# Gate and experts through tangents on ScalarE, and four more of 64 products with C on VectorE

## The chip, the cores and the metric

The kernel runs on one core of a Trainium2 chip. The metric is the device time of one execution in microseconds (us). Engines are named as the profile names them: PE is TensorE's matmul, PEld its weight load, DVE is VectorE, ACT is ScalarE, POOL is GpSimd, SP is SyncE, whose queue issues the transfers.

## The reference, cut to what matters

One layer of a decoder in three parts, each with a layer norm ahead of it and a residual sum behind it, on x of 64 x 128 x 512 floats: a state-space mixer, a banded cross attention, and a layer of eight experts. The mixer and the experts hold the silus that the change touches:

```
proj = einsum('blh,ph->blp', x, in_proj_w); h_in, gate = split(proj, 2)
u = silu(conv(h_in) + conv_b)                       # 1024 channels, 4 taps
ts, Bm, Cm = split(einsum('bli,pi->blp', u, x_proj_w))
dt = softplus(einsum('blr,ir->bli', ts, dt_proj_w) + dt_proj_b)
h[t] = exp(dt[t] * A) * h[t-1] + dt[t] * u[t] * Bm[t]    # 16 states a channel
y = einsum('blin,bln->bli', h, Cm) + D * u
y = y * silu(gate)
x = x + einsum('bli,hi->blh', y, out_proj_w)
...
h = einsum('bth,eih->beti', x, down_w)
a = silu(h)                                         # 8 experts of 16 units
out = einsum('beth,bte->bth', einsum('beti,ehi->beth', a, up_w), top2_gate)
```

## The kernel before

The 64 batch rows are worked off in 32 groups g of two rows (GB = 2). Every engine has a list written out by hand, `iteration(g, cur, nxt, p1, p2)`, which holds four things at once: the scan part of the mixer for group g (`cur`), the preparation of group j = g + 1 (`nxt`: layer norm, input products, taps, u, time step), the attention of group g - 1 (`p1`) and the experts of group g - 2 (`p2`). Engines meet only through semaphores, so an instruction that waits holds up all that stands behind it in its own list. A loop runs two iterations at a time; the first, the second and the last ones are written out, `first_iteration` and `last_iteration` among them.

The scan part of a group has 64 steps s. Step s is channel block ic = s // 8 (128 channels) and state pair r = s % 8; it works on 128 x 512 floats (two states, two rows, 128 time steps):

- `decays(g, s)` on ACT (L564): two exponents of delta times A into one of two PSUM banks (DAR = 2). The soft steps (softplus) use the same two banks in turn. `bank_free` lets it wait until the bank's last user is done: the scan (`h_done`), or, where the product with C is DVE's, that product (`hcd_done`). In that case ACT must also write the first columns anew (L561).
- `times_b(g, s)` on POOL (L351): du times B into one of eight slots of `ring`; it waits until PE has summed what stood in the slot (`hc_used`), at a group's start also for `du_done` and for the transfer `bc_in`.
- `scan(g, s)` on DVE (L1789): the recurrence. Its result goes into the ring, or for steps in `DVE_C` into the PSUM bank.
- `times_c`: the product with C, on POOL for most steps (L360), on DVE (L1773) for those in `DVE_C`, now 16 of 64: s % 8 in (1, 5).
- `y_sum(g, s)` on PE (L1321): transposes two finished slots and adds them up in bank PS_Y; `y_step` on DVE (L1782) multiplies the sum of a channel block by the gate; `y_turn` on PE (L1342) transposes it back into PS_B, and `y_back` on ACT (L658) copies it to `yz`, which `out_proj` (L1351) uses.

Bank PS_B is shared, one user at a time: `h_in` (L1371) with `tap3` on ACT and `conv` on DVE (L1895), `gate_in` (L1394) with the gate's copy, `dt_in` (L1429), `ts_in`, `bc_in_rows`, `transposed_x` and `y_turn`. Each next user waits on PE for the semaphore of the last reader. For the gate that is `gate_done`, which `h_in`, `transposed_x`, `dt_in` and `y_turn` wait for.

Today the gate (quarters q = 0 to 3 of its channels) is copied raw by `gate_raw` (L683) and turned in two halves by `gate_silu` (L689) beside the silus of u (L676). The experts' silu is L743, their product with the weights L1795. `soft_step` 1 to 4 on DVE (L1757 to L1768) with `soft_exp`, `soft_one`, `soft_ln`, `soft_back` on ACT make softplus; step 4 makes `du`. The tiny powers of the layer norms are POOL's (L339), the shifts that use them DVE's (L1745).

## Time and profile before

| | us |
|---|---|
| median of 3 runs | 4900.89 (4900.83 to 4907.75) |
| profiled execution | 4886.05 |
| its span | 4884.2 |

| engine | busy us | share of the span |
|---|---|---|
| PE | 4537.1 | 93% |
| PEld | 3339.0 | 68% |
| POOL | 4505.7 | 92% |
| ACT | 4281.4 | 88% |
| DVE | 4252.6 | 87% |

Busy time is the union of an engine's instructions in one profiled execution. The ends of matmuls are modelled, so a busy PE may hold waits. The span runs from the first to the last instruction. Releasers are inferred from semaphore events: a wait is put down to the instruction that signalled last. Since the kernel repeats one group 32 times, most of what there is to see is in one group, and windows are cut at the first product of a group on POOL.

### The profile page before, as it was taken

The page shows a single profiled execution, that of the slowest core. Times are in us where ns is not written, and L with a number is a line of the kernel's source. Part 1 is how long each engine was busy: PE and PEld are TensorE (multiplying, and loading weights), DVE is VectorE, ACT ScalarE, POOL GpSimd, SP SyncE. Part 2 cuts the span into 40 slices and gives each one's busy share as a digit, 9 for nine tenths or more (in the row PEclk, how much of TensorE's full clock was granted, in tenths as well). Part 3 has the DMA queues.
Part 4 walks back from the last instruction along what each step waited for, and adds up shares of the span by engine and source line. Part 5 has one row for each costly group of instructions (what it writes and reads, how often), then busy time and mean ns, then how long its engine had stood idle before and what let it go on. Part 6 is the DMA issues. An engine that isn't in the chain of part 4 may idle for free.

```text
span 4884.2 us, 142078 instructions
## 1 busy us (share of the span) xinstructions
PE 4537.1 (93%) x52548; PEld 3339.0 (68%) x52548; DVE 4252.6 (87%) x5795; ACT 4281.4 (88%) x9026; POOL 4505.7 (92%) x3726
## 2 busy tenths in 40 slices
PE   5799999999999999999999999999999999999977
PEld 4576767776767776767767676777667777677754
DVE  3788989899988899988899988899989899888883
ACT  5788999988999988999988999988999989999873
POOL 3999999999999999999999999999999999999991
PEclk8899999999999999999999999999999999999999
DMA  3211222212222212222212222212222212222200
GB/s 127 80 55 64 77 80 79 84 49 73 77 79 80 84 47 75 77 79 79 84 40 82 77 79 80 84 38 84 77 80 79 84 35 88 77 79 80 71 8 19
DMA packets 119316, 350.46 MB, mean 72 GB/s; under 512 B 18688, under 2 KB 19456, under 8 KB 118528
## 3 DMA queue, kind: packets, MB, share of 16 engines
q1 hardware_dynamic: 118656, 341.51, 20.3%
q8 instruction: 432, 7.08, 0.6%
q14 instruction: 228, 1.87, 0.1%
HBM read 323.64 MB, written 17.83 MB: 70 GB/s over the span
## 4 chain that ended last, share of the span: by engine, by line
PE 41%; POOL 34%; issue 12%; DVE 8%; DMA 2%; ACT 1%; POOLq 0%; SPq 0%; DVEq 0%; ACTq 0%
POOL ring L351 21%; POOL ring L360 12%; PE ps L1321 8%; PE ps L1371 7%; PE ps L1394 6%; DVE ring L1789 3%; PE ps L1351 3%; DMA bc<-bc_rows 2%; PE ps L1210 2%; PE ps L1276 2%; PE ps L1265 2%; PE ps L1237 2%; DVE nmax L1813 2%; PE ps L1301 2%; DVE hc L1895 1%
## 5 line engine op out<-in xcount | busy, mean ns | idle before, releaser
L351 POOL TENSOR_TENSOR ring<-du,bc 128x512 f32<-128x512 f32 x2048 | 2581.9, 1288 | 205.1 <-PE ps L1321 109.4
L360 POOL TENSOR_TENSOR ring<-ring,bc 128x512 f32<-128x512 f32 x1536 | 1947.2, 1290 | 48.3 <-DVE ring L1789 42.4
L1789 DVE TENSOR_TENSOR_SCAN ring<-ps,ring 128x512 f32<-128x512 f32 x1536 | 1828.8, 1211 | 184.3 <-ACT ps L564 154.3
L564 ACT ACTIVATE ps<-delta,a_neg 128x254 f32<-128x254 f32 x4096 | 1760.7, 469 | 159.2 <-DVE ring L1789 150.4
L1321 PE MATMUL ps<-ident,ring 128*128 128x128 f32 x8192 | 1073.8, 277 | 54.2 <-POOL ring L360 51.7
L1321 PEld LDWEIGHTS ps<-ident,ring 128*128 128x128 f32 x8192 | 914.8, 142 | 208.2 <-issue 140.4
L1789 DVE TENSOR_TENSOR_SCAN ps<-ps,ring 128x512 f32<-128x512 f32 x512 | 622.7, 1216 | 70.7 <-ACT ps L564 47.8
L1371 PE MATMUL ps<-xt_a,w_in 128*128 128x256 f32 x2048 | 477.0, 386 | 16.6 <-ACT yz L658 14.8
L1394 PE MATMUL ps<-w_in,xt_a 128*128 128x256 f32 x2048 | 472.6, 384 | 4.2 <-ACT delta L617 3.0
L726 ACT ACTIVATE probs_mem<-ps 128x768 f32<-128x768 f32 x504 | 443.1, 912 | 30.4 <-PE ps L1265 21.4
L1351 PE MATMUL ps<-w_outp,yz 128*128 128x512 f32 x1024 | 465.8, 593 | 2.7 <-issue 1.5
L1371 PEld LDWEIGHTS ps<-xt_a,w_in 128*128 128x128 f32 x2048 | 382.5, 192 | 82.3 <-ACT yz L658 22.5
L1394 PEld LDWEIGHTS ps<-w_in,xt_a 128*128 128x128 f32 x2048 | 384.1, 191 | 77.5 <-issue 24.2
L1895 DVE SCALAR_TENSOR_TENSOR hc<-ps,conv_w,hc 128x254 f32<-128x254 f32 (+2 forms) x768 | 362.2, 475 | 46.1 <-ACT hc L669 26.1
L1813 DVE TENSOR_REDUCE nmax<-ps 128x8 f32<-128x1280 f32 x252 | 371.5, 1474 | 30.5 <-PE ps L1237 29.0
L1773 DVE TENSOR_TENSOR ring<-ps,bc 128x512 f32<-128x512 f32 x512 | 350.3, 684 | 8.0
L1351 PEld LDWEIGHTS ps<-w_outp,yz 128*128 128x128 f32 x1024 | 182.4, 190 | 173.3 <-issue 171.5
L1237 PE MATMUL ps<-qk 32*32 32x160 f32 (+2 forms) x16128 | 289.5, 295 | 0.0
L1265 PE MATMUL ps<-qk 32*128 32x192 f32 x4032 | 262.0, 374 | 0.0
L1210 PE MATMUL ps<-xb,w_qk 128*128 128x512 f32 x504 | 241.8, 602 | 11.9 <-ACT xb L595 11.7
L1276 PE MATMUL ps<-probs_mem,v_aug 128*32 128x192 f32 x4032 | 218.9, 358 | 14.5 <-ACT probs_mem L726 14.3
L1237 PEld LDWEIGHTS ps<-qk 32*32 32x32 f32 x16128 | 198.0, 103 | 37.3 <-issue 0.6
(174 smaller groups left out, 6280.7 us busy)
## 6 DMA issues: line engine op xcount, KB each, us to landing
w_in<-in_w_in SPq DMA_DIRECT2D x256, 512.0 KB, 3.6
bc<-bc_rows SPq DMA_DIRECT2D x256, 512.0 KB, 5.9
x_new<-in_x SPq DMA_DIRECT2D x32, 512.0 KB, 8.1
x_res<-in_x SPq DMA_DIRECT2D x32, 512.0 KB, 7.6
out<-x_att SPq DMA_DIRECT2D x32, 512.0 KB, 2.9
enc<-in_ctx SPq DMA_DIRECT2D x63, 256.0 KB, 3.4
w_outp<-in_w_outp SPq DMA_DIRECT2D x1, 2048.0 KB, 7.9
bc_rows<-bc_sb SPq DMA_DIRECT2D x128, 8.0 KB, 1.4
```

Source lines behind the costliest of these rows:

```text
L351: nc.gpsimd.tensor_tensor(ring[:, s % RING, :].rearrange("p (n t) -> p n t", n=2), du[:, q % 2, (ic % 2) * NT:(ic % 2 + 1) * NT].rearrange ...
L360: nc.gpsimd.tensor_tensor(ring[:, s % RING, :], ring[:, s % RING, :], bc[:, s % RS, 2:4, :].rearrange("p a t -> p (a t)"), ALU.mult).then_ ...
L564: nc.scalar.activation(ps[:, bank("step", s), (n % 2) * NT:(n % 2 + 1) * NT].rearrange("p (b t) -> p b t", b=GB)[:, :, 1:T], delta[:, ic, ...
L726: nc.scalar.activation(L.probs[:, :, blk, lo:hi], ps[:, L.bank:L.bank + 4, (n % 2) * WIN + lo:(n % 2) * WIN + hi], ACT.Exp).then_inc(L.p_d ...
L1237: last = nc.tensor.matmul(ps[32 * a:32 * a + 32, L.bank + hp, j * NEAR + lo:j * NEAR + hi], L.qk[r:r + 32, j, n * P + 32 * a:n * P + 32 * ...
L1321: last = nc.tensor.matmul(ps[:, PS_Y, b * T:(b + 1) * T], ring[:, t % RING, n * NT + b * T:n * NT + (b + 1) * T], ident[:], start=False, s ...
L1351: last = nc.tensor.matmul(ps[:, PS_ATT + b, :], yz[:, ic, b * T:(b + 1) * T], w_outp[:, ic, :], start=(ic == 0), stop=(ic == NI - 1))
L1371: last = nc.tensor.matmul(ps[:, prep_bank(j, "h", q), a * NT:(a + 1) * NT], w_in[:, slot, k, a * P:(a + 1) * P], xt_a[:, k, :], start=(k = ...
L1394: last = nc.tensor.matmul(ps[:, PS_B, b * NT:(b + 1) * NT], xt_a[:, k, b * T:(b + 1) * T], w_in[:, slot, k, :], start=(k == 0), stop=(k == ...
L1789: nc.vector.tensor_tensor_scan(state, ps[:, bank("step", s), :], ring[:, s % RING, :], 0.0, ALU.mult, ALU.add).then_inc(h_done, 1)
L1813: nc.vector.tensor_reduce(L.nmax[:, n].rearrange("p j (a r) -> p a j r", r=32)[:, :, :, DH], ps[:, L.bank:L.bank + 4, 0:NJ * NEAR].rearran ...
L1895: nc.vector.scalar_tensor_tensor(acc[:, :, s:T], src[:, :, 0:T - s], conv_w[:, ic, KC - 1 - s:KC - s], acc[:, :, s:T], ALU.mult, ALU.add). ...
```

## The change

1. The gate: `gate_raw` and `gate_silu` go. ACT's `gate_tanh(j, q)` writes tanh(gate / 2) from PS_B into `gate_t`, and DVE's new `gate_half(j, q)` makes (tanh + 1) * gate from it and PS_B. That is twice the silu, so `y_back` halves it. `gate_done` is now signalled by `gate_half`.
2. The experts: `experts_tanh` and `experts_half` in the same way, and `experts_gated` carries the factor 0.5.
3. `DVE_C` has 20 of 64 steps, s % 16 in (1, 5, 9, 11, 13), in place of 16: steps 11, 27, 43 and 59 move from POOL to DVE.
4. The lists of POOL, ACT, PE and DVE are ordered anew. SP's list is the same.

```diff
-    DVE_C = [s for s in range(64) if s % 8 in (1, 5)]
+    DVE_C = [s for s in range(64) if s % 16 in (1, 5, 9, 11, 13)]
...
-                nc.scalar.copy(yz[:, ic, :], ps[:, PS_B, 0:NT]).then_inc(yz_done, 1)
+                nc.scalar.activation(yz[:, ic, :], ps[:, PS_B, 0:NT], ACT.Identity, scale=0.5).then_inc(yz_done, 1)
...
-            def gate_raw(j, q):
+            def gate_tanh(j, q):
 
                 reached(act, y_done, (j - 1) * NI + 2 * q + 2)
                 act.wait_ge(gin_ps, j * NQ + q + 1)
-                nc.scalar.copy(gate_t[:, :, 2 * q * P:(2 * q + 2) * P],
-                               ps[:, PS_B, :].rearrange("p (b c) -> p b c", b=GB)).then_inc(gate_done, 1)
-
-            def gate_silu(g, h):
-                act.wait_ge(gate_done, g * NQ + 2 * h + 2)
-                z = gate_t[:, :, 4 * h * P:4 * (h + 1) * P]
-                nc.scalar.activation(z, z, ACT.Silu).then_inc(gate_act, 1)
+                nc.scalar.activation(gate_t[:, :, 2 * q * P:(2 * q + 2) * P],
+                                     ps[:, PS_B, :].rearrange("p (b c) -> p b c", b=GB), ACT.Tanh, scale=0.5).then_inc(gate_act, 1)
...
-                nc.scalar.activation(act_e, ps[:, PS_ATT + 2, 0:NT], ACT.Silu).then_inc(act_done, 1)
+                nc.scalar.activation(act_e, ps[:, PS_ATT + 2, 0:NT], ACT.Tanh, scale=0.5).then_inc(act_tanh, 1)
...
+            def gate_half(j, q):
+
+                dve.wait_ge(gate_act, j * NQ + q + 1)
+                z = gate_t[:, :, 2 * q * P:(2 * q + 2) * P]
+                nc.vector.scalar_tensor_tensor(z, z, 1.0, ps[:, PS_B, :].rearrange("p (b c) -> p b c", b=GB),
+                                               ALU.add, ALU.mult).then_inc(gate_done, 1)
+
...
-                dve.wait_ge(gate_act, g * 2 + ic // 4 + 1)
+                dve.wait_ge(gate_done, g * NQ + ic // 2 + 1)
...
+            def experts_half(g):
+
+                dve.wait_ge(act_tanh, g + 1)
+                nc.vector.scalar_tensor_tensor(act_e, act_e, 1.0, ps[:, PS_ATT + 2, 0:NT], ALU.add, ALU.mult).then_inc(act_done, 1)
+
...
-                nc.vector.tensor_tensor(gated, ps[:, PS_ATT + 3, 0:NT], act_e, ALU.mult).then_inc(gated_done, 1)
+                nc.vector.scalar_tensor_tensor(gated, ps[:, PS_ATT + 3, 0:NT], 0.5, act_e, ALU.mult, ALU.mult).then_inc(gated_done, 1)
```

Of the lists, what the prediction speaks of. Start of an iteration on POOL (in the new order the power "e" of group g - 2 stands behind three products) and on DVE (y_step 7 comes first, the shifts later):

```diff
                 if cur:
                     times_b(g, 0)
-                if p2:
-                    rstd("e", g - 2, 0, 2)
-                if p1:
-                    second_lane(g)
-                if cur:
                     times_b(g, 1)
                     times_b(g, 2)
+                if p2:
+                    rstd("e", g - 2, 0, 2)
...
-                if p2:
-                    shift("e", g - 2, 0)
+                if p1:
+                    y_step(g - 1, 7)
                 if cur:
                     scan(g, 0)
                     scan(g, 1)
                 if p2:
-                    shift("e", g - 2, 1)
+                    shift("e", g - 2, 0)
```

The end of an iteration on DVE:

```diff
                 if p1:
                     attention(g, 1, "x2")
+                if cur:
+                    scan(g, 63)
                 if nxt:
                     soft_step(1, j, 0)
-                if cur:
-                    scan(g, 63)
-                if nxt:
                     soft_step(2, j, 0)
                     soft_step(3, j, 0)
                     soft_step(4, j, 0)
+                    gate_half(j, 2)
```

On DVE the new instructions stand so: `gate_half(g, 3)` between soft step 4 of quarter 1 and scan 6; `experts_half` between the two parts of `router`; `gate_half(j, 0)` between soft steps 1 and 2 of quarter 3, behind `times_c` 33; `gate_half(j, 1)` between scan 43 and the third maximum of lane 1; the products with C of steps 11, 27, 43 and 59 behind mixer_add 1, y_step 2, the third maximum and scan 59. On ACT, `gate_tanh(g, 3)` stands ahead of decays 6, `gate_tanh(j, 0)` behind `soft_one(g, 3)`, `gate_tanh(j, 1)` right ahead of the silus of u, and `gate_tanh(j, 2)` behind `soft_ln(j, 0)`, with the next exponents behind it.

## Rows read from the trace of the kernel before

**Rows 1.** The page: busy time by engine, and the chain that ended last by engine.
```profile
PE 4537.1 (93%) x52548; PEld 3339.0 (68%) x52548; DVE 4252.6 (87%) x5795; ACT 4281.4 (88%) x9026; POOL 4505.7 (92%) x3726
...
PE 41%; POOL 34%; issue 12%; DVE 8%; DMA 2%; ACT 1%; POOLq 0%; SPq 0%; DVEq 0%; ACTq 0%
```

**Rows 2.** Busy by stage: stretch, length, PE, PEld, DVE, ACT, POOL; clock; DMA.
```profile
4772.00:4884.00 112.00, 86.10 (x1178) 50.77 (x1178) 34.60 (x77) 42.78 (x68) 7.09 (x10) 0.92 0.06 20
...
sum 1174.70, PE 1121.90 PEld 827.93 DVE 1061.41 ACT 1068.28 POOL 1125.53; mean PE 140.24 PEld 103.49 DVE 132.68 ACT 133.54 POOL 140.69
...
2175.00:2228.00 53.00, 51.74 (x634) 39.46 (x626) 49.53 (x68) 46.27 (x94) 48.75 (x41) 1.00 0.14 41
```

**Rows 3.** Waits of POOL in eight groups, 1396 to 2570.7: total us, times, longest.
```profile
POOL ring L351 <- PE ps L1321: 27.0, 24, 1.6
POOL ring L360 <- DVE ring L1789: 11.4, 16, 1.3
POOL ring L351 <- DVE du L1768: 8.4, 9, 0.9
```

**Rows 4.** Waits of DVE in the same eight groups.
```profile
DVE ring L1789 <- ACT ps L564: 34.5, 37, 2.9
DVE ln_nm_e L1745 <- POOL ln_rs_e L339: 17.7, 8, 2.2
...
DVE ps L1789 <- ACT ps L564: 11.3, 16, 0.8
```

**Rows 5.** Timeline over one group: POOL's products, and last three scans on DVE.
```profile
2129.71 1.27 POOL L351 TENSOR_TENSOR ring<-du,bc 128x512 f32<-128x512 f32 x1 [0.94 <-DVE du L1768]
...
2131.60 6.19 POOL L351 TENSOR_TENSOR ring<-du,bc 128x512 f32<-128x512 f32 x5
...
2276.36 1.27 POOL L351 TENSOR_TENSOR ring<-du,bc 128x512 f32<-128x512 f32 x1 [0.94 <-DVE du L1768]
...
2219.16 3.45 DVE L1789 TENSOR_TENSOR_SCAN ring<-ps,ring 128x512 f32<-128x512 f32 x3
```

**Rows 6.** Groups of instructions, whole run: count, busy us, mean ns, idle before.
```profile
L360 POOL TENSOR_TENSOR ring<-ring,bc 128x512 f32<-128x512 f32 x1536 | 1947.2, 1290 | 48.3 <-DVE ring L1789 42.4 <-PE ps L1321 4.6 <-issue 1.3
L1789 DVE TENSOR_TENSOR_SCAN ring<-ps,ring 128x512 f32<-128x512 f32 x1536 | 1828.8, 1211 | 184.3 <-ACT ps L564 154.3 <-POOL ring L351 27.0
...
L1773 DVE TENSOR_TENSOR ring<-ps,bc 128x512 f32<-128x512 f32 x512 | 350.3, 684 | 8.0
...
L561 ACT COPY ps<-zeros 128x4 f32<-128x4 f32 x640 | 105.3, 164 | 18.0 <-DVE ring L1773 16.5
...
L633 ACT ACTIVATE ps<-soft 128x512 f32<-128x512 f32 x128 | 76.3, 596 | 5.8 <-DVE ring L1789 2.8
...
L683 ACT COPY gate_t<-ps 128x512 f32<-128x512 f32 x128 | 73.2, 572 | 7.5 <-PE ps L1394 7.4
...
L689 ACT ACTIVATE gate_t<-gate_t 128x1024 f32<-128x1024 f32 x64 | 63.9, 1048 | 0.0
...
L1831 DVE SCALAR_TENSOR_TENSOR o_sb<-ps,enc 128x512 f32<-128x512 f32 x63 | 43.0, 682 | 26.9 <-PE ps L1301 26.9
...
L743 ACT ACT_TABLE_LOAD x32 | 41.1, 1283 | 0.6
...
L564 ACT ACT_TABLE_LOAD x157 | 201.4, 1283 | 2.8
```

**Rows 7.** Timeline of ACT in the same group: gate copy, silus of the gate, load back.
```profile
2205.14 0.59 ACT L683 COPY gate_t<-ps 128x512 f32<-128x512 f32 x1
...
2226.88 1.99 ACT L689 ACTIVATE gate_t<-gate_t 128x1024 f32<-128x1024 f32 x2
...
2228.95 1.28 ACT L564 ACT_TABLE_LOAD   x1
```

**Rows 8.** Chain of waits in order of time: start, us, what (PE, same group).
```profile
2199.49 3.46 PE ps L1394 x16
...
2206.49 3.46 PE ps L1371 x16
```

More of the change, by code:

```diff
@@ L961, in iteration @@
                     u_silu(j, 3)
+                if cur:
+                    y_back(g, 4)
+                    decays(g, 51)
+                    decays(g, 52)
                 if p1:
@@ L1629, in iteration @@
                 if p1:
+                    attention(g, p2, 1, "rep")
+                if nxt:
+                    dt_in(j, 2, cur)
+                if p1:
+                    attention(g, p2, 1, "wo")
+                if cur:
+                    y_sum(g, 59)
+                    y_turn(g, 6, nxt)
+                if p1:
                     attention(g, p2, 1, "ct")
-                if cur:
-                    y_turn(g, 6, nxt)
-                    y_sum(g, 59)
                 if nxt:
@@ L2055, in iteration @@
                 if cur:
-                    times_c(g, 41)
-                    scan(g, 42)
+                    y_step(g, 4)
+                    scan(g, 43)
+                if nxt:
+                    gate_half(j, 1)
                 if p1:
```

537 lines of the change are left out of this document (258 added, 279 removed).

## The prediction

> **What bounds the kernel now.** The page comes first: four engines are busy for 87 to 93% of the span, and the chain that ended last lies 41% on PE and 34% on POOL [rows 1]. No single engine stands out there, because the start and the end of the run are in the average. So the second view is the busy time by stage, cut at the starts of the groups on POOL. The reader is to see that a group of two batch rows takes 146.8 us (1174.70 over 8), with POOL 140.7, PE 140.2, ACT 133.5 and DVE 132.7 us busy in it, and that only the last 112 us are of another kind [rows 2]. The timeline of POOL confirms the period: the first product of two consecutive groups starts at 2129.71 and at 2276.36 [rows 5]. 32 groups make 32 x 146.8 = 4698 us of the 4884; the rest is start and tail.
>
> The third view is who POOL waits for. Over eight groups it is 27.0 + 11.4 + 8.4 us, under 6 us a group: PE freeing a ring slot, DVE ending a scan, DVE ending `du` [rows 3]. POOL's own work is fixed: five products in a row take 6.19 us and one takes 1.27, so they start (6.19 - 1.27) / 4 = 1.23 us apart [rows 5], and 112 of them a group (64 with B, 48 with C) are 137.8 us. So POOL runs from product to product nearly without a break and is the bound of the steady stretch. PE is a close second: between 2175 and 2228 us it is busy for 51.7 of 53 us [rows 2]. But PE's ends are modelled, and its stretches with waits count in part as busy, so I take its 140.2 as an upper bound of its need.
>
> The fourth view is who DVE waits for: it idles 14.1 us a group, of which (34.5 + 11.3) / 8 = 5.7 us are scans that wait for ScalarE's decays and 2.2 us the shift that waits for POOL's power at the start of a group [rows 4].
>
> **The change, part by part, for one group.**
>
> *POOL loses four products with C* (steps 11, 27, 43, 59): 4 x 1.23 = 4.9 us, 140.7 - 4.9 = 135.8. As POOL is the bound, all of it lies on the path until another engine takes over.
>
> *DVE gets those four*, at 0.68 us each (L1773) [rows 6]: 2.7 us. The scan before each writes to PSUM and not to the ring, which I cost at nothing. It gets four `gate_half`, 128x512 from SBUF and PSUM. The nearest row is the product with the context, the same form and size, 0.68 us (L1831) [rows 6]: 2.7 us. And it gets one `experts_half`, half the size: between half of L1831 and the whole, 0.34 to 0.68; I take 0.4. Together 5.9 us by durations. Three scans in a row take 3.45 us and not 3 x 1.21 [rows 5], so each instruction behind another costs some 0.09 less than its duration: 9 x 0.09 = 0.8 off, and 5.1 is the other end. I take 5.7: DVE goes from 132.7 to 138.4.
>
> *ScalarE loses* two `gate_silu` of 1.05 us, 2.1 (L689), and the two table loads about the experts' silu, one before it (L743, 32 in the run, one a group) and one back to the exponent (L564, 157 in the run, five a group): 2 x 1.28 = 2.6 [rows 6]. The gate's silus sat between loads that `u_silu` needs anyway, so those stay. It gains next to nothing where a copy becomes an activation: four times 572 to at most 596 ns (L683, L633), 0.1; eight `y_back` likewise, 0.1 to 0.2. And it must set the first column of the decays' bank four more times, after each new product on DVE: 4 x 0.16 = 0.7 (L561) [rows 6]. ScalarE: 133.5 - 4.7 + 0.9 = 129.7.
>
> In this trace a load costs its 1.28 us and no more: the load back at 2228.95 stands right behind the gate's silus, which began at 2226.88 and ran 1.99 us, to 2228.87 [rows 7], and the 32 loads ahead of the experts' silu have 0.6 us of idle time in front of them in all [rows 6]. So the sum goes by 1.28. The Trainium skill, "ScalarE: Activation LUTs", What ACT_TABLE_LOAD costs, adds a drain of about 1.38 us to each switch of tables, by which the two switches would be worth an estimated 5.3 us and ScalarE would stand near 127. The trace disagrees with it.
>
> *The waits that are added.* The gate's sum must now stay in PS_B until DVE has multiplied it, where ScalarE's copy freed the bank before. `gate_done` is DVE's now, and PE's next user of the bank (`h_in`, `transposed_x`, `dt_in`, `y_turn`) waits for it. Queued behind a waiting `gate_half` on DVE are the scans, behind them POOL's products with C. The price of each is at least the 0.68 us of the instruction on the bank's chain and at most that and one scan in front of it, 1.9 us; four a group, 2.7 to 7.6 us on PS_B. What hides it is PE's other work (attention and `y_sum` use other banks), and with that cover I take nothing; without it the full price lands on PE. The new product on DVE also holds a PSUM bank of decays for 0.68 + 0.16 us longer before ScalarE can fill it. In the order on DVE something stands between each such pair (a maximum, an addition, a `y_step`), which covers it. A gain from these waits is excluded, since they only hold banks longer.
>
> *The order.* On DVE scan 63 now stands ahead of all four soft steps, where one stood ahead of it: the first product of the next group waits for `du` 0.94 us now [rows 5], and scan 63 and the steps come in the same total, so I expect 0 to 0.7 us more. POOL's power "e" moves behind three products and DVE's shift moves behind two scans, which gives back a part of the 2.2 us wait [rows 4]. These cancel, within 1 us. On SP nothing is moved; its spreads wait for the same steps' last use, 59 now on DVE. Start and tail: no silu of the gate in the first group, `gate_in` 2 later there, one table load fewer in the tail; between -2 and +2 us in all, taken as 0.
>
> **The sum.** The heaviest engine falls from POOL's 140.7 to DVE's 138.4, with POOL at 135.8 right below. The bound engine now idles 146.8 - 140.7 = 6.1 us a group. If the new one idles as long, the period is 138.4 + 6.1 = 144.5, which is 2.3 us less; 32 x 2.3 = 74 us. That asks DVE's idle time to fall from 14.1 to 6.1 us, and 5.7 of that are waits for ScalarE, which has lost 3.8 us of work and the two longest interruptions in their present size. The profiled execution took 4886.05 us around a span of 4884.2; 4886 - 74 = 4812. The median of the runs stands 14.8 us above the profiled one, so the forecast for the median is **4826 us**.
>
> **The rivals.**
>
> *POOL's saving comes through whole.* For it: DVE and ScalarE are waited for by POOL little today (19.8 us in eight groups [rows 3]), and DVE's 138.4 still fits under 141.9. Against: DVE would have 3.5 us of idle time a group, where it has 14.1. Time: 32 x 4.9 = 157, 4901 - 157 = 4744. Chance 0.17.
>
> *Nothing comes of it.* Of DVE's 14.1 us of idle time, 8.4 are not waits for ScalarE. If these are not slack but real latencies (PE to maximum, POOL to shift), the period is 138.4 + 8.4 = 146.8, as today; PE's full stretch from 2175 to 2228 us would end the same way, since PE loses no work. Time: 4901. Chance 0.10.
>
> *Slower, through the bank PS_B.* The place is PE's full stretch. `gate_in` of gate 0 starts there at 2199.49 and runs 3.46 us; `h_in` 2, the next user of the bank, starts at 2206.49 [rows 8], and ScalarE's copy between them ran from 2205.14 to 2205.73 [rows 7], 0.8 us ahead of it. A `gate_half` behind the tangent takes the bank to 2206.4 at best, and to 2207.6 with a scan in front of it; gate 1 falls into the same stretch and is taken as equally tight. In this stretch PE's halts go through to POOL, which already waits most for PE [rows 3]. At the upper price the two gates cost 2 x 1.9 = 3.8 us a group, while the saving of 2.3 is felt only in the other 94 of 147 us, 1.5. So it decides from 0.75 us a gate, and in full it gives 2.3 us more a group: 4901 + 74 = 4975. Against it: PE's other banks give it work, if the order puts it there. Chance 0.10.
>
> *The tangent doesn't share the decays' table.* Then the change doesn't do what it says: each lone tangent brings a load in and one back. Gate 0, gate 3 and the experts stand alone, six loads, and gate 2 between logarithm and exponent makes one more; above the forecast's count that is 7 x 1.28 = 9 us a group, 129.7 + 9.0 = 138.7 on ScalarE, beside a DVE of 138.4 that waits for it. With ScalarE's idle time of 146.8 - 133.5 = 13.3 us kept, the period is 152.0: 4901 + 32 x 5.2 = 5067. No row has a tangent, so none decides; other functions, such as the reset and the gate's copy (L561, L683) [rows 6, 7], run among the exponents without a load, while silu and logarithm bring one. Chance 0.04. The Trainium skill, "ScalarE: Activation LUTs", Table sets: the hidden batching unit, lists tanh in the set of exp, by which no load is added; no row of this trace shows it.
>
> **How the numbers follow.** The forecast's own case has 0.59, with a range of its own of 4773 to 4879 (DVE at 137.8 to 138.6, idle time of the bound engine 5 to 7.5 us, so a period of 142.8 to 146.1). The whole range goes from 4740, which takes in the first rival, to 4905, which takes in "nothing comes of it"; outside are the two slow cases, 0.14, and the tails of the others. A measurement of this kernel can tell about 0.2%, 10 us, from no change. Faster: 0.59 + 0.17 = 0.76, and 0.01 of "nothing comes of it", which leaves 0.09 for the same; slower: 0.10 + 0.04 = 0.14.
>
> **What would show it.** In the profile after: L360 with 1408 products instead of 1536, DVE's product with C with 640; POOL at 135.8 us a group; ScalarE's loads down by 64 in all and its busy time near 130; DVE near 138.4 and the largest of the three. Right is the forecast if DVE's waits for ScalarE fall to some 2 us a group and POOL's idle time rises to 8 or 9. It is wrong if POOL's waits for PE grow (the bank), if DVE shows long waits ahead of `gate_half`, or if loads appear at the tangents' line.

## The result, and the profile after

The kernel after takes 4931.38 us (median of 4 runs, 4930.73 to 4933.95), the one before 4900.86: a ratio of 1.007 (95% interval 1.0054 to 1.0085). It is slower, and outside the range of the prediction. In the profiled executions the spans are 4928.9 and 4884.2 us, 44.7 apart; the profiled execution of before was some 15 us shorter than its median, so these rows show about 15 us more than the medians do.

Those 15 us go with TensorE's granted clock. The profiled execution of before has a mean of 0.989. Of 62 further executions of before, made beside the runs below, five stand at 0.988 and took 4882 to 4894 us; 0.985 is the commonest value, with 4893 to 4905 us; three stand at 0.983, with 4901 to 4907. So the usual execution of before loses time to the clock that its trace does not show. The kernel after took 4931 to 4934 us at 0.982 to 0.983. At a like clock the change costs some 25 us, an estimate (4931 against 4907 at 0.983), and only the other 5 or 6 of the 30.5 come from a clock that is lower than before's usual one.

The page of the kernel after: busy time, the chain that ended last, and the groups that answer to [rows 6].

```profile
PE 4565.9 (93%) x52548; PEld 3373.7 (68%) x52548; DVE 4397.6 (89%) x6083; ACT 4184.7 (85%) x9025; POOL 4353.3 (88%) x3598
...
PE 44%; DVE 17%; POOL 16%; issue 14%; ACT 7%; DVEq 0%; DMA 0%; POOLq 0%; ACTq 0%; SPq 0%
...
L351 POOL TENSOR_TENSOR ring<-du,bc 128x512 f32<-128x512 f32 x2048 | 2566.6, 1278 | 302.8 <-PE ps L1299 191.9
L360 POOL TENSOR_TENSOR ring<-ring,bc 128x512 f32<-128x512 f32 x1408 | 1778.0, 1278 | 128.4 <-DVE ring L1772 127.1
...
L1749 DVE TENSOR_TENSOR ring<-ps,bc 128x512 f32<-128x512 f32 x640 | 437.8, 684 | 8.0
...
L558 ACT COPY ps<-zeros 128x4 f32<-128x4 f32 x768 | 126.8, 165 | 122.2 <-DVE ring L1749 117.5
```

The counts are those of the change (1408 and 640 products with C), and POOL, 34% of the chain in [rows 1], is down to 16%, while DVE went from 8 to 17%. Lines shifted: the scan is L1772 now, the decays L561, `y_sum` L1299, `gate_half` L1757, the tangent L680.

Busy time by stage, cut at the starts of groups on POOL, as in [rows 2]: two groups of eight, and the sum.

```profile
1848.30:1997.60 149.30, 141.76 (x1643) 105.29 (x1642) 137.18 (x190) 130.52 (x283) 135.94 (x112) 0.99 0.22 74
1997.60:2145.40 147.80, 140.36 (x1643) 103.62 (x1642) 137.34 (x190) 130.68 (x283) 136.00 (x112) 1.00 0.22 73
...
sum 1188.20, PE 1128.47 PEld 835.62 DVE 1097.83 ACT 1045.14 POOL 1087.84; mean PE 141.06 PEld 104.45 DVE 137.23 ACT 130.64 POOL 135.98
```

A group takes 148.5 us, where it took 146.8 [rows 2]. The work of each engine is close to the forecast: POOL 136.0 (135.8), DVE 137.2 (138.4), ScalarE 130.6 (129.7), PE 141.1 (140.2, as before). POOL's load fell by 4.7 us and the group got longer. But the heaviest load hardly fell: it is PE's now, 140.3 in the short groups, where POOL's was 140.7. So the error lies in the idle time, and in which engine counts as the bound. And the groups alternate, 149.3 and 147.8, with 1.4 us more busy time on PE in the long ones.

Who waits in these eight groups of the kernel after (1254.3 to 2442.5), answering to [rows 3, 4]: total us, times, longest.

```profile
POOL ring L351 <- PE ps L1299: 47.9, 43, 2.4
POOL ring L360 <- DVE ring L1772: 33.4, 45, 1.7
POOL ring L351 <- DVE du L1744: 14.3, 8, 1.8
...
DVE ring L1772 <- ACT ps L561: 34.6, 36, 2.2
DVE gate_t L1757 <- ACT gate_t L680: 11.5, 16, 0.8
DVE ps L1772 <- ACT ps L561: 10.9, 8, 1.6
...
PE ps L1159 <- DVE nmax L1801: 16.7, 16, 1.7
```

POOL's waits grew by three quarters for PE (27.0 to 47.9), tripled for DVE's scans (11.4 to 33.4) and rose for `du` (8.4 to 14.3). DVE's waits for the decays are what they were: 34.6 + 10.9 against 34.5 + 11.3. PE's waits for a maximum come to the same total as before, but in 16 pieces of up to 1.7 us and not 32 of up to 1.0; this row of the kernel before (1396 to 2570.7) is:

```profile
PE ps L1181 <- DVE nmax L1813: 17.4, 32, 1.0
```

The long groups are explained by TensorE's clock. Busy time of after in stretches of 3.4 us, some 39 us into a long group (the last three columns are the granted clock, the DMA share and GB/s).

```profile
2177.80:2181.20 3.40, 3.31 (x86) 2.69 (x88) 3.40 (x7) 3.37 (x9) 3.02 (x3) 1.00 0.18 67
2181.20:2184.60 3.40, 1.66 (x96) 0.99 (x75) 3.40 (x4) 3.24 (x8) 3.40 (x4) 1.00 0.27 96
2184.60:2188.00 3.40, 3.40 (x37) 3.14 (x16) 3.40 (x4) 2.15 (x5) 3.40 (x4) 0.50 0.00 0
```

And PE in the timeline of the same place:

```profile
2180.51 1.17 PE L1215 MATMUL ps<-qk 32*32 32x128 f32 x64
2183.42 0.32 PE L1159 MATMUL ps<-band,ident 32*128 32x320 bf16 x4 [1.74 <-DVE nmax L1801]
```

PE waits 1.74 us for a maximum, is busy for 1.66 of 3.40 us, and right behind that the granted clock is 0.50, so 1.2 instead of 2.4 GHz, for 3.4 us. In the trace of after this happens in 14 of 27 steady groups; in that of before never. The wait itself is in all 27 groups, 1.74 to 1.75 us each time, so the wait alone does not decide whether the clock falls.

### The profile page after: what moved, and what is told of

It is laid out like the page before. It is cut to its first block, busy times and chain, and to the rows that moved or that the text cites. A ratio compares the mean times of both kernels' runs of the same rounds, so it can differ in the third digit from the quotient of the medians.

```text
span 4928.9 us, 142489 instructions
## 1 busy us (share of the span) xinstructions
PE 4565.9 (93%) x52548; PEld 3373.7 (68%) x52548; DVE 4397.6 (89%) x6083; ACT 4184.7 (85%) x9025; POOL 4353.3 (88%) x3598
## 4 chain that ended last, share of the span: by engine, by line
PE 44%; DVE 17%; POOL 16%; issue 14%; ACT 7%; DVEq 0%; DMA 0%; POOLq 0%; ACTq 0%; SPq 0%
POOL ring L351 10%; PE ps L1299 8%; PE ps L1349 7%; POOL ring L360 6%; PE ps L1372 5%; PE ps L1215 4%; DVE ring L1772 4%; DVE ps L1772 3%; PE ps L1243 3%; PE ps L1254 2%; PE ps L1188 2%; DVE nmax L1801 2%; PE ps L1329 2%; ACT ps L561 2%; DVE ring L1749 1%
## 5 line engine op out<-in xcount | busy, mean ns | idle before, releaser
L360 POOL TENSOR_TENSOR ring<-ring,bc 128x512 f32<-128x512 f32 x1408 | 1778.0, 1278 | 128.4 <-DVE ring L1772 127.1
L561 ACT ACTIVATE ps<-delta,a_neg 128x254 f32<-128x254 f32 x4096 | 1757.4, 467 | 134.1 <-DVE ring L1772 122.5
L1772 DVE TENSOR_TENSOR_SCAN ring<-ps,ring 128x512 f32<-128x512 f32 x1408 | 1671.4, 1211 | 152.4 <-ACT ps L561 143.8
L1299 PE MATMUL ps<-ident,ring 128*128 128x128 f32 x8192 | 1080.8, 280 | 36.0 <-POOL ring L360 32.5
L1299 PEld LDWEIGHTS ps<-ident,ring 128*128 128x128 f32 x8192 | 948.7, 144 | 114.5 <-issue 100.1
L1772 DVE TENSOR_TENSOR_SCAN ps<-ps,ring 128x512 f32<-128x512 f32 x640 | 778.2, 1216 | 52.7 <-ACT ps L561 49.7
L1749 DVE TENSOR_TENSOR ring<-ps,bc 128x512 f32<-128x512 f32 x640 | 437.8, 684 | 8.0
L558 ACT COPY ps<-zeros 128x4 f32<-128x4 f32 x768 | 126.8, 165 | 122.2 <-DVE ring L1749 117.5
```

What stands on the lines that cost most here:

```text
L360: nc.gpsimd.tensor_tensor(ring[:, s % RING, :], ring[:, s % RING, :], bc[:, s % RS, 2:4, :].rearrange("p a t -> p (a t)"), ALU.mult).then_ ...
L561: nc.scalar.activation(ps[:, bank("step", s), (n % 2) * NT:(n % 2 + 1) * NT].rearrange("p (b t) -> p b t", b=GB)[:, :, 1:T], delta[:, ic, ...
L1299: last = nc.tensor.matmul(ps[:, PS_Y, b * T:(b + 1) * T], ring[:, t % RING, n * NT + b * T:n * NT + (b + 1) * T], ident[:], start=False, s ...
L1749: nc.vector.tensor_tensor(ring[:, s % RING, :], ps[:, bank("step", s), :], bc[:, s % RS, 2:4, :].rearrange("p a t -> p (a t)"), ALU.mult). ...
L1772: nc.vector.tensor_tensor_scan(state, ps[:, bank("step", s), :], ring[:, s % RING, :], 0.0, ALU.mult, ALU.add).then_inc(h_done, 1)
```

## The experiments

Two theories from the comparison. **T1**: the tangents hold the bank PS_B for DVE, and PE, nearly full, loses what it waits (the prediction's third rival). **T2**: POOL was not the only bound; its relief turns into waits, and what is lost comes from the order of the work and what it does to PE (the clock). "Group" is the mean of the steady groups 3 to 29 of the profiled execution; "falls" is how many falls of the clock those 27 groups hold; the last column is the mean of those of the 27 that hold none, and how many they are. Each ratio is against the executions of before that were made beside that run, whose medians lie between 4896.5 and 4901.9 us.

The expectations name their theories anew. BANK is T1; ORDER, CLOCK and LATENCY are forms of T2; and "theory DVE" is a third, that every microsecond of work given to DVE lengthens the group.

| run | median us | ratio to before (95%) | group us | falls | us without a fall |
|---|---|---|---|---|---|
| before | 4900.9 | 1 | 146.80 | 0 | 146.80 (27) |
| after | 4931.4 | 1.0070 (1.0054 to 1.0085) | 148.55 | 14 | 147.86 (13) |
| tangents_alone | 4980.3 | 1.0167 (1.0147 to 1.0187) | 149.71 | 1 | 149.64 (26) |
| c20_alone | 4903.1 | 1.0011 (1.0002 to 1.0021) | 147.26 | 0 | 147.26 (27) |
| tangents_c20_old_order | 5046.6 | 1.0310 (1.0293 to 1.0327) | 152.06 | 9 | 151.50 (18) |
| after_c16 | 5060.5 | 1.0329 (1.0307 to 1.0351) | 152.51 | 32 | 150.77 (5) |
| new_lists_silus | 5194.5 | 1.0601 (1.0584 to 1.0619) | 156.99 | 54 | none |
| experts_tangent | 4899.3 | 1.0000 (0.9989 to 1.0010) | 147.19 | 5 | 146.78 (22) |
| after_no_dip | 4984.0 | 1.0174 (1.0153 to 1.0195) | 150.09 | 2 | 150.06 (25) |
| after_filled | 4911.6 | 1.0031 (1.0018 to 1.0043) | 147.77 | 0 | 147.77 (27) |
| before_light_pe | 4866.0 | 0.9929 (0.9909 to 0.9948) | 146.22 | 24 | 144.60 (3) |
| after_light_pe | 4860.1 | 0.9922 (0.9905 to 0.9938) | 146.08 | 17 | 145.36 (10) |
| tangents_light_pe | 4848.3 | 0.9897 (0.9880 to 0.9915) | 145.78 | 1 | 145.67 (26) |
| c20_light_pe | 4970.9 | 1.0143 (1.0118 to 1.0167) | 150.02 | 77 | none |
| after_short_half | 4927.5 | 1.0059 (1.0042 to 1.0076) | 148.43 | 13 | 147.74 (14) |
| after_light_short | 4838.0 | 0.9871 (0.9855 to 0.9887) | 145.70 | 16 | 144.90 (11) |
| after_no_silu_load | 4905.6 | 1.0017 (1.0006 to 1.0028) | 147.67 | 13 | 147.05 (14) |
| before_no_silu_load | 4891.8 | 0.9988 (0.9978 to 0.9997) | 147.00 | 4 | 146.70 (23) |
| filled_c59_back | 4915.3 | 1.0045 (1.0029 to 1.0062) | 147.78 | 0 | 147.78 (27) |
| filled_c59_scan63 | 4932.2 | 1.0078 (1.0058 to 1.0098) | 148.26 | 0 | 148.26 (27) |

Of the 18 runs behind the first two, five came out in a range that was named for them (experts_tangent, tangents_c20_old_order, after_light_pe, after_short_half, before_no_silu_load) and two within 5 us of a named time (after_filled, filled_c59_back). The other eleven lie outside every range named, so neither theory had the sizes right.

### The parts of the change, each by itself

**The tangents in the order of before.** The functions of the change, each `gate_half` at its place among DVE's old neighbours, 16 products with C (on ScalarE the second tangent stands one place earlier than the copy did, ahead of the first silu of u):

```diff
-                    gate_raw(j, 0)
+                    gate_tanh(j, 0)
...
-                    gate_silu(g, 1)
-                if nxt:
-                    gate_silu(j, 0)
...
                     scan(g, 43)
+                if nxt:
+                    gate_half(j, 1)
```

> Kernel of before with its own lists and its own 16 products with C on DVE; only the silus of gate and experts become tangents with gate_half and experts_half. Theory DVE (each microsecond of work given to DVE lengthens the group, whatever the others lose): DVE 132.7 + 3.0, ScalarE 133.5 - 4.3, POOL stays at 140.7, so the group stays within 1 us of 146.8, 4880 to 4930. Theory ORDER (the parts are good, the new lists lose the time): ScalarE's two loads fewer shorten the waits of the scans, and the group falls by 0.5 to 1.5 us, 4855 to 4885.

They cost 1.7%. Waits of PE in eight groups of tangents_alone (1276.5 to 2473.2):

```profile
PE ps L1361 <- DVE gate_t L1771: 18.6, 16, 1.6
PE ps L1171 <- DVE nmax L1815: 18.1, 32, 1.0
```

`h_in`, the next user of PS_B, waits for `gate_half` twice a group, 18.6 / 8 = 2.3 us, of the 2.9 us by which the group is longer. That is T1, at the place that the prediction's third rival names and inside its price of 1.9 us a gate. How much of it is the hold of the bank and how much the place of `gate_half` behind other work of DVE, no run separates: `gate_half` was never shortened in this order.

**The four products in the order of before** (each behind its scan on DVE, gone from POOL's list):

```diff
-    DVE_C = [s for s in range(64) if s % 8 in (1, 5)]
+    DVE_C = [s for s in range(64) if s % 16 in (1, 5, 9, 11, 13)]
```

> Kernel of before with silus as they are and its own lists; only the products with C of steps 11, 27, 43 and 59 go from POOL to DVE, each right behind its scan. Theory DVE: POOL 140.7 - 4.9, DVE 132.7 + 2.7 = 135.4, the scans wait longer for decays that wait for the product: group 147 to 149 us, 4905 to 4970. Theory ORDER: the bound engine gets 4.9 us shorter and the group falls by 1 to 3 us, 4805 to 4870.

Busy time and POOL's waits of c20_alone in eight groups (1251.3 to 2429.3):

```profile
sum 1178.00, PE 1122.42 PEld 827.54 DVE 1080.97 ACT 1071.51 POOL 1086.93; mean PE 1122.42 PEld 827.54 DVE 1080.97 ACT 1071.51 POOL 1086.93
...
POOL ring L351 <- PE ps L1317: 56.8, 36, 2.6
POOL ring L360 <- DVE ring L1785: 25.9, 32, 1.2
```

POOL is at 1086.93 / 8 = 135.9 us, 4.8 less, and not one microsecond comes out: the group is 0.5 us longer. POOL's waits grew from 27.0 + 11.4 to 56.8 + 25.9, by 44.3 / 8 = 5.5 us a group. So POOL was no bound by itself: other chains are as long. T2's first half is shown. The ratio of 1.0011 flatters the run: it has no fall and a clock of 0.988 to 0.990 in its executions, which took 4899 to 4907 us, where before took 4882 to 4894 at 0.988.

**Both in the order of before.** The change without its new order:

> The kernel before with the whole change but its order: tangents, gate_half behind what they need, C products of steps 11, 27, 43, 59 on VectorE right behind their scans, all else as before. Tangents alone cost 79 us and the four products alone 2. Theory 1, the loss is in the hold of the bank PS_B, which the products don't touch: 4980 to 4990. Theory 2, the two add up worse, because DVE gets both works and gate_half then waits behind a product with C too (0.7 us a gate more on the bank's chain): 5000 to 5080. Rival, POOL's relief takes up a part of the tangents' loss: 4930 to 4960, and then the new order is worth nothing; by theories 1 and 2 it is worth 50 to 150 us.

The two add up to more than their sum: 3.1% against 1.7 + 0.1. So the new order is worth 5047 - 4931 = 115 us against this kernel. It is not the cause of the loss as a whole, it hides most of it. It does so at the bank too: here PE waits for `gate_half` 102 us at `h_in` over the whole run, and in after once there, for 0.7 us, and three times in all:

```profile
PE ps L1407 <- DVE gate_t L1757: 2.8, 1, 2.8
PE ps L1349 <- DVE gate_t L1757: 0.7, 1, 0.7
PE ps L1372 <- DVE gate_t L1757: 0.3, 1, 0.3
```

**The new order without one part.** The four products given back to POOL (11 behind B 17, the others beside their neighbours with C):

> Kernel after with the four products with C back on POOL (steps 11, 27, 43, 59, each put where a free ring slot needs it), all else as after. POOL 140.9, DVE 134.6. Theory DVE: no gain is lost with the four, the group comes back to 146 to 148 us, 4880 to 4925. Theory ORDER: POOL's work comes on top of the stalls that the new lists make, group 149 to 152, 4945 to 5040.

And the silus back in the new order, with `gate_raw` at the tangents' places and `gate_silu` twice behind `u_silu`:

> Kernel after with its new lists and its 20 products with C on DVE, but gate and experts with silus as before (gate_raw at the places of gate_tanh, the two gate_silu behind the silus of u). DVE 135.4, ScalarE 134.2, POOL 135.8. Theory BANK: the new lists are made to cover the hold of PS_B, so without it they gain little, and ScalarE's loads come back: 4920 to 4960. Rival, theory DVE: 3 us less on DVE shorten the group by 1 to 3 us, 4835 to 4900.

Both are far slower than after. In after_c16 PE's `y_sum` waits for POOL's products, which it hardly did:

```profile
PE ps L1303 <- POOL ring L360: 24.3, 16, 2.2
```

In the new order the four products are worth 129 us, and nothing in the old one. A part of it is TensorE's clock, which falls 32 and 54 times in the 27 groups of these two. So the products have no price of their own outside an order.

The other run says less. In new_lists_silus DVE's `y_step` waits for the silu of the gate, 24.6 and, put down to "issue", 24.2 us in eight groups (1300 to 2556), 6.1 us a group, and in before it did not:

```profile
DVE yg L1768 <- ACT gate_t L686: 24.6, 4, 6.2
DVE yg L1768 <- issue: 24.2, 4, 6.1
```

In this run that silu stands behind decays 44, in before behind decays 42. So its 5.3% over after are in large part the place that the silu was given, and whether the new order suits silus stays open.

**The experts' tangent alone**, in the order of before:

> Kernel of before with its lists; only the experts' silu becomes a tangent on ScalarE and experts_half on DVE, so the two table loads go and the bank PS_B, which only the gate uses, is held no longer. Theory BANK (the tangents lose by the longer hold of PS_B alone: with them PE waits 2.3 us a group for gate_half): no loss here, ScalarE 2.6 us lighter, the group within 0.5 us of 146.8 or a little under, 4880 to 4905. Theory DVE (any work added to DVE lengthens the group): 0.4 us more a group, 4910 to 4920.

Two loads and their 2.6 us leave ScalarE in each group, and the time is the same (1.0000). Its groups without a fall take 146.8 us, as in before. But it has five falls, in the order of before, so falls belong to that order too, though the trace of before has none. One of them, with the stretch ahead of it and what PE waited for there:

```profile
1571.40:1574.80 3.40, 2.50 (x17) 2.03 (x17) 3.33 (x8) 2.78 (x7) 3.40 (x3) 1.00 0.00 0
1574.80:1578.20 3.40, 3.40 (x10) 2.04 (x9) 3.19 (x16) 2.42 (x7) 3.40 (x5) 0.50 0.00 0
...
1573.94 2.99 PE L1210 MATMUL ps<-xb,w_qk 128*128 128x512 f32 x4 [0.90 <-ACT xb L595]
```

This run, at 4897.9 us and a clock of 0.986, is what a usual execution of before may look like; no trace of one was taken.

### TensorE's clock

**y_sum 11 between the scores**, so that PE has work while it waits for the maximum:

```diff
                     attention(g, p2, 0, "v")
-                if cur:
-                    y_sum(g, 11)
-                if p1:
                     attention(g, p2, 0, "s", 0)
+                if cur:
+                    y_sum(g, 11)
+                if p1:
                     attention(g, p2, 0, "s", 1)
```

> Kernel after with one change in PE's list: y_sum 11 stands between the first and the second block of scores of lane 0 again, as in the kernel before, so that PE has work while it waits 1.7 us for the maximum on DVE. In after the granted clock falls to half for 3.4 us once in two groups right behind that wait, and those groups take 149.3 us and not 147.8. Theory CLOCK: the dips go, every group takes 147.8, 16 x 1.5 = 24 us less than after, 4907. Rival: the longer group of each pair is the loop's own (before had 146.3 and 147.5 without any dip), so 0 to 8 us less, 4923 to 4931.

The clock stays up (2 falls), and the kernel is 1% slower than after: in eight groups PE's `y_sum` now waits 17.8 us for POOL's products, and POOL's waits for PE rise to 59.1 us from 47.9. A swap is no clean test of the clock.

**Fillers in the wait**, which move nothing:

```diff
                     else:
+                        if n == 1 and b == 0 and L is lanes[0]:
+                            for _ in range(12):
+                                nc.tensor.matmul(ps[:, PS_Y, 256:384], ident[:], ident[:], start=True, stop=True, is_transpose=True, skip_group_check=True)
                         pe.wait_ge(L.max_done, i * 4 + n)
```

> The kernel after, with 12 transposes of the identity into an unused corner of PE's bank for y, put ahead of PE's wait for the maximum of scores 1 of lane 0: PE is kept busy in the wait (1.7 us) behind which the granted clock fell to 0.50 for 3.4 us once every two groups. Nothing else moves, and no order changes. If the dip of the clock costs what PE's lost half speed is worth, 1.5 us in every second group, 16 x 1.5 = 24 us come back: 4907, with a mean group of 147.8. If the dip lies beside other waits, the time is 4931 as after. If the fillers are longer than the wait they cost up to 0.1 us each, 12 x 0.05 x 32 = 20 us at the most: 4951.

(The output of this kernel is not the layer's; with the same fillers issued without a start, as in the last two kernels below, it is. The work is the same.) PE's waits for a maximum fall from 16.7 to 5.0 us in eight groups:

```profile
PE ps L1159 <- DVE nmax L1804: 5.0, 16, 0.3
```

All groups are now 147.6 to 148.0 us. The ratio goes from 1.0070 to 1.0031: 0.39%, 19 us. So the falls of the clock cost the kernel after 19 us. They are not two thirds of the 30 by which it is slower, since before's usual execution loses some 15 us with a lower clock too. At 0.988 and above, after_filled took 4908 to 4914 us in five executions and before 4882 to 4894: some 25 us are left. Elsewhere a group with one is longer by a similar amount: 153.2 against 151.5 us in tangents_c20_old_order, 1.7.

### PE's full stretch

**Half the sum over the inputs left out in `h_in` and `gate_in`**, which takes 10 us a group off PE's busy time in before (140.2 to 130.1), and some 12 in the two kernels behind it:

```diff
-                    for k in range(KH):
+                    for k in range(KH // 2):
```

> Kernel of before with half of the sum over the model's width left out in h_in and gate_in (two of four chunks), which takes 32 x 0.216 x 2 = 13.8 us of PE's work a group away and shortens each hold of PS_B by 1.7 us. The output is not the layer's. Theory PE (PE's full stretch sets the pace with POOL): the group falls from 146.8 towards POOL's own 140.7 plus what it waits for scans and du, 143 to 145, 4785 to 4840. Rival (POOL alone sets it): 146 to 147, 4870 to 4900.

> Kernel after with the same half of h_in and gate_in left out. Output not the layer's. Theory PE: what POOL, with 135.8 us of work, could not show behind PE's full stretch shows now; the group falls from 148.5 below that of the lightened kernel of before, 141 to 143, 4715 to 4790. Theory DVE: DVE's 137.2 us of work with 11 us of waits for decays and for gate_half stay, 146 to 148.5, 4850 to 4930.

> The kernel before with only the tangents, in its own order, and with half of the sum over the inputs left out in h_in and gate_in (the mixer's inputs are wrong by that). Tangents alone cost 79 us beside 4901 with PE's waits for gate_half at h_in of 2.3 us a group. If that loss is the hold of the bank in PE's full stretch, it is gone or below 20 us where PE has slack: 4866 to 4886. If the loss was from DVE's added work (3.1 us a group) or from the order of gate_half ahead of the scans, it stays: 4930 to 4950.

By the medians the difference of before and after is gone (0.9929 and 0.9922), and the tangents' 79 us have turned into a gain: 4848 against 4866. But the three have 24, 17 and 1 falls. Their groups without a fall take 144.6 us in before_light_pe (three groups alone), 145.4 in after_light_pe and 145.7 in tangents_light_pe. So with PE light the tangents cost 1.1 us a group and not 2.8 (149.64 - 146.80), and the whole change 0.8 and not 1.1 (147.86 - 146.80). Of tangents_light_pe, waits of PE in eight groups (1237.4 to 2401.9), and the sum of busy time:

```profile
PE ps L1361 <- DVE gate_t L1771: 18.6, 16, 1.6
...
PE ps L1419 <- DVE gate_t L1771: 13.7, 8, 1.8
...
sum 1164.50, PE 1026.94 PEld 727.88 DVE 1077.94 ACT 1033.48 POOL 1124.39; mean PE 1026.94 PEld 727.88 DVE 1077.94 ACT 1033.48 POOL 1124.39
```

PE waits for `gate_half` at `h_in` just as long (18.6 us) and at `dt_in` besides (13.7), and all of it costs some 1.1 us a group where PE has 128.4 us of work in 145.6; at 140.8 in 149.6 the wait at `h_in` alone came with 2.8. So the price of the tangents hangs on how full PE is, as T1 says; the 1.1 rest on three groups of before_light_pe. In before 10 us less on PE take 2.2 us off a group without a fall, while 4.8 us less on POOL took nothing: PE's work was in the period, and POOL's was not by itself.

> The kernel before with only the four products moved to VectorE, and with half of the sum over the inputs left out in h_in and gate_in (256 of the matmuls of a pair of groups less; the mixer's inputs are wrong by that). It stands against the kernel before with the same matmuls left out, 4866 us, a group 146.2. If it was PE that swallowed POOL's 4.9 us, they come out here: 3 to 4.9 us a group, 4710 to 4770. If the chain of DVE and ScalarE is as long as POOL's, as the waits for decays say, little comes out: 4840 to 4866. If both share it, between: 4770 to 4840.

Above every case. The clock fell 77 times in 27 groups, almost three times a group, so this run tells of the clock and not of who swallowed POOL's saving. That stays open between PE and the chain of DVE and ScalarE.

**`gate_half` cut to 8 of its 512 elements a partition** (the gate is then wrong in the rest), alone and with the light PE:

```diff
-                nc.vector.scalar_tensor_tensor(z, z, 1.0, ps[:, PS_B, :].rearrange("p (b c) -> p b c", b=GB),
+                nc.vector.scalar_tensor_tensor(z[:, :, 0:4], z[:, :, 0:4], 1.0, ps[:, PS_B, :].rearrange("p (b c) -> p b c", b=GB)[:, :, 0:4],
```

> Kernel after with each gate_half cut from 512 to 8 elements a partition; its waits and signals stay, so 4 x 0.6 = 2.4 us of DVE's work a group go and PS_B is held 0.6 us less each time. Output not the layer's. Theory LATENCY (what sets the group is the ring of decays on two banks, scans and products on DVE, with PE's stretch in the middle, and each has its own waits): part of the 2.4 us comes through, 0.8 to 2 us a group, 4865 to 4905. Theory DVE PACE (DVE's work is the sum that counts): all 2.4 comes through, 4840 to 4855. Rival, PE alone: nothing, 4925 to 4935.

> Kernel after with both cuts, half of h_in and gate_in left out on PE and gate_half on 8 elements. Output not the layer's. Theory LATENCY: with PE light the group is 146.1 and DVE's chain alone sets it; 2.4 us less work on DVE comes through nearly whole, 143.5 to 144.5, 4780 to 4810. If POOL or ScalarE set it there, it stays at 4850 to 4860.

In the new order `gate_half`'s duration hardly matters: 4927 against 4931, the intervals overlap. So T1's cost is covered there, as PE's waits for `gate_half` in after said, and what is lost is elsewhere. With PE light it is worth 0.5%, and there POOL waits mostly for DVE's scans, 46.7 us in eight groups of after_light_pe, beside 12.3 for PE.

### ScalarE's loads

**The silus of u, and in before those of the gate too, computed as tangents** (u is then another function), which takes four loads a group away:

> Kernel after with the silus of u computed as tangents without a product, so that the four table loads about them go, 5.1 us of ScalarE a group. Output not the layer's. Theory LATENCY: the scans' long waits for decays stand right behind those loads (2.2 and 1.3 us a group), and go: 2 to 3.5 us a group less, 4820 to 4870. Rival (PE's stretch or POOL sets the group): under 0.5 us, 4915 to 4930.

> Kernel of before with the silus of u and gate computed as tangents without a product, so that the same four table loads go. Output not the layer's. If POOL is the bound of before, which waits only 6 us a group, little comes: 0 to 1.5 us a group, 4850 to 4900. If the chain of decays and scans is as long as POOL's work there too and both must fall, also little, so this run tells only whether it is more than 2 us (4835 and below), which would mean POOL was never the bound.

Stretch of eight groups and DVE's waits in after_no_silu_load (1254.8 to 2438.9):

```profile
1254.80:2438.90 1184.10, 1129.59 (x13138) 836.89 (x13137) 1098.07 (x1520) 1004.72 (x2225) 1087.31 (x897) 0.99 0.22 73
...
DVE ring L1772 <- ACT ps L561: 26.1, 28, 1.6
...
DVE ps L1772 <- ACT ps L561: 11.6, 8, 1.5
```

ScalarE has 125.6 us of work, 5.1 less, and a group is 0.9 us shorter (0.8 in those without a fall); in before the same edit takes 0.1% off. DVE's waits for the decays fell by only 1 us a group. So most of them do not hang on ScalarE's total. Its own waits for a product of DVE to free a bank rose meanwhile, from 24.6 to 38.3 us in eight groups:

```profile
ACT ps L558 <- DVE ring L1749: 38.3, 56, 2.0
```

### What is left without the falls

After_filled is still 1.0 us a group above the trace of before, and neither has a fall. In its timeline DVE runs with hardly a break (0.15 us) into `du` at a group's end while POOL waits:

```profile
2131.71 1.27 POOL L360 TENSOR_TENSOR ring<-ring,bc 128x512 f32<-128x512 f32 x1 [1.31 <-DVE ring L1775]
2133.50 1.28 POOL L360 TENSOR_TENSOR ring<-ring,bc 128x512 f32<-128x512 f32 x1 [0.51 <-DVE ring L1775]
2136.57 3.73 POOL L351 TENSOR_TENSOR ring<-du,bc 128x512 f32<-128x512 f32 x3 [1.79 <-DVE du L1747]
```

So the product 59 went back to POOL, and in a second kernel scan 63 also went back behind soft step 1 (the fillers are now issued without a start):

```diff
+                if nxt:
+                    soft_step(1, j, 0)
                 if cur:
                     scan(g, 63)
                 if nxt:
-                    soft_step(1, j, 0)
                     soft_step(2, j, 0)
```

> The kernel after with the 12 filler transposes ahead of PE's wait for the maximum (now added to an unused corner of the bank without clearing it), and with the product with C of step 59 given back to POOL, behind that of step 58: DVE computes 19 of 64. Fillers alone gave a group of 147.77 us. In its last 17 us DVE is busy without a break but POOL waits 1.31, 0.51 and 1.79 us for it, so DVE is the bound there, and the product 59 lies in that stretch. If that is so, 0.6 to 0.7 us a group come back, 20 us: 4890. If the product is simply worth the same on either engine there, 4911. If POOL is as tight as in the other stretches, it costs 1.23 us a group: 4950.

> As the run before, and DVE's scan 63 stands behind soft step 1 again, as in the kernel before, where the change put it ahead of all four. POOL's first product of a group then waits for du 0.94 us (before) and not 1.79 (after): if this wait sets the start of the group, up to 0.85 us a group, 27 us, come back: 4863, which beats both kernels. If the same work of DVE stands ahead of du in either order (scan 63 lies ahead of it both times), du ends at the same instant and nothing changes: as the run before, within 5 us.

The first comes out as if the product were worth the same on either engine, the second misses. The group stays at 147.78 with the product on either engine, although POOL's waits for scans fell by 10 us in eight groups. With scan 63 back, the wait for `du` leaves the list of POOL's waits, and the group is 0.5 us longer, with more waits for PE: 53.1 us against 41.2 in filled_c59_back.

```profile
POOL ring L351 <- PE ps L1303: 53.1, 48, 2.1
POOL ring L360 <- DVE ring L1776: 30.2, 40, 1.4
```

In the second, a wait of POOL that was taken away at one place came back at others; in the first 10 us fewer of waits changed nothing. So POOL's waits, as such, do not set the period here. No kernel with all its work in place is faster than before by more than a measurement can tell.

## Why the prediction was wrong

- **The work of each engine**: right within 1.2 us a group. DVE's addition was 4.5 us, though, under the 5.1 to 5.9 of the prediction. The table loads are right too: 320 in before, 255 in after. The tangent comes among the exponents without a load (L680 has 31, those of gate 2 behind the logarithm), so the rival with the tables is out. The Trainium skill, "ScalarE: Activation LUTs", Table sets: the hidden batching unit, lists tanh beside exp, and by these counts the trace agrees.
- **A load costs 1.28 us and no drain**: holds in after, in ScalarE's timeline of the end of a group:

```profile
2141.29 1.28 ACT L641 ACT_TABLE_LOAD   x1
2142.58 1.06 ACT L641 ACTIVATE lnv<-soft 128x1024 f32<-128x1024 f32 x1
...
2144.06 1.28 ACT L680 ACT_TABLE_LOAD   x1
2145.36 0.60 ACT L680 ACTIVATE gate_t<-ps 128x512 f32<-128x512 f32 x1
```

  The logarithm starts 1.29 us after the start of its load, which took 1.28. The Trainium skill, "ScalarE: Activation LUTs", What ACT_TABLE_LOAD costs, adds a drain of about 1.38 us; the trace disagrees, there is 0.01 us between the two.
- **"As POOL is the bound, all of it lies on the path"**: the step that failed first. c20_alone: 4.8 us less work, 5.5 us more waits, a ratio of 1.0011, a group 0.5 us longer. POOL idled 6.1 us a group and PE 6.6, and the prediction took the first for the bound and let the second go.
- **"The heaviest engine falls from POOL's 140.7 to DVE's 138.4"**: failed on the prediction's own numbers, since PE, with 140.2, loses no work and is heavier than DVE. For a period of 144.5 PE's idle time would have had to fall to 4.3 us. Its rival "nothing comes of it" named this, with a chance of 0.10. Measured: PE 140.3 of 147.8 us in the groups without a fall.
- **"With that cover I take nothing", of the waits on PS_B**: held, but only by the order. In the old order the tangents cost 2.8 us a group, by the mechanism of the third rival: PE waits 2.3 us for `gate_half` at `h_in`, and with PE light the cost falls to some 1.1. In the new order, which the prediction was about, the cover came: PE waits for `gate_half` three times in the whole run, and shortening it changes nothing that can be told.
- **"The order: within 1 us"**: failed, in a way not thought of. The new order brings PE a wait of 1.7 us where it had at most 1.0, and TensorE's clock falls behind it in every second group, which costs 19 us (shown by after_filled). Against before's usual execution, which loses some 15 us with its clock, that is about 5 of the 30. It also moved PE's, DVE's and POOL's waits about, which is a gain of 115 us against the old order with the same work.
- **"If the new one idles as long", 6.1 us**: failed, and it is the term that was mis-sized. DVE idled 148.5 - 137.2 = 11.3 us a group. Its waits for the decays stayed at 5.7 us, where the forecast asked for some 2; after_no_silu_load shows that even 5 us less on ScalarE takes only 1 us from them.
- **Start and tail at 0**: the three first groups took 5.6 us less, the first began 3.7 us later, the tail was 3.2 us shorter, 5 us less in all where it allowed 2. It is no part of the loss.
- **The signs** of an error that it named: one of three came, POOL's waits for PE grew, though not through the bank. Waits ahead of `gate_half` were short (0.8 us at most), and the 31 loads at the tangents' line stand in place of loads at the next exponents.

So the gain that was forecast is missing because POOL was not the bound; that is shown. Why the kernel is slower than before is shown only for the falls of the clock. What stays open: the 1.0 us a group, some 25 us, between after_filled and before at a like clock, for which two edits on DVE and POOL were no answer (c20_alone has 0.5 of it, in the old order), and whether PE or DVE's chain took POOL's 4.9 us.

## What to carry to other kernels

Where four engines are each busy for 90 to 96% of a period, relieving the busiest gained nothing by itself here: list every engine's load after the change, those that lose no work too, and test the relief alone before tying an order to it. An instruction inserted between a PSUM bank's producer and its next user is priced at the engine that owns the next use: with PE busy for 141 of 150 us the tangents cost 2.8 us a group, at 128 of 146 some 1.1. When an order is changed, lay the granted clock of both traces side by side: a new fall behind a wait of PE is a cost that no sum of work shows. And compare at a like clock: one profiled execution with a clock above the usual made before look 15 us better than its median.

## What the runs showed of the hardware

- A wait of PE of 1.74 us between score matmuls stands in all 27 steady groups of after, and in 14 of them 3.4 us at half clock followed, which made those groups 1.3 to 1.5 us longer (149.2 against 147.9 in the mean). In the trace of before waits of up to 1.0 us at the same line were not followed by one. But in experts_tangent, in before's order, the clock fell five times some 26 us into a group, once behind a wait of 0.90 us, and in before_light_pe a wait of 2.11 us passed without a fall. So no length of a single wait decides it. Twelve transposes ahead of the wait kept the clock up, and cost less than they gave (4912 against 4931 us).
- Less work on PE can make the kernel slower. With half of the sum over the inputs left out, 10 us of PE's 140.2 in a group, the clock fell 24 times in before's steady groups, whose trace had none, and 77 times in c20_light_pe, which took 4971 us where c20_alone, with all its work, took 4903.
- One kernel's executions differ by their granted clock: before took 4882 to 4894 us at 0.988 and 4901 to 4907 at 0.983.
